# Taking the products of zeros out of the first microseconds of a one-core graph kernel

## What is computed

```python
edge_index = jnp.stack([src, dst])
x = _layernorm(x + _L0_gnn_ref(x, edge_index, ...))          # (x@W+b) spread three times over a 0/1 adjacency
x = _layernorm(x + _L1_gnn_ref(x, W, b, src, dst, 1024))     # sum of neighbours @ W.T + b
x = _layernorm(x + _L2_gnn_ref(x, wc, wn, bias, edge_index)) # x@wc + mean of (x@wn) over the edges + bias
x = _layernorm(x + _L3_gnn_ref(x, edge_index, ...))          # 8 heads of attention with softmax per target
```

## Time and profile before

| | |
|---|---|
| median of three executions | 392.14 us (391.53 to 392.75) |
| the profiled execution's own time | 390.91 us |
| its span, first to last instruction | 389.1 us |
| TensorE busy | 371.8 us (96%) |
| VectorE busy | 280.7 us (72%) |
| ScalarE busy | 239.8 us (62%) |
| GpSimd busy | 100.7 us (26%) |

### The profile page before, as it was taken

One profiled execution on the slowest core, in us unless ns is written; L12 is line 12 of the kernel. 1 busy time (PEld: TensorE's weight loads), 2 busy tenths in 40 slices (PEclk: granted clock), 3 DMA queues, 4 the chain that ended last, 5 costly groups with the idle time before them and its releaser, 6 DMA issues.

```text
span 389.1 us, 7789 instructions
## 1 busy us (share of the span) xinstructions
PE 371.8 (96%) x2721; PEld 218.3 (56%) x2721; DVE 280.7 (72%) x598; ACT 239.8 (62%) x415; POOL 100.7 (26%) x93
## 2 busy tenths in 40 slices
PE   6999989999999999999999999999899999999990
PEld 2455556544444444444444444444458889999990
DVE  8899999659986774207755446553795978999984
ACT  9999977575812355203661111467776999999344
POOL 5102000098800368100891000367200000112110
PEclk9999989999999999999999999999999999999997
DMA  5960060033000000000352000034202111210005
GB/s 166 385 221 1 0 217 3 3 109 107 2 0 0 0 2 3 0 2 0 72 91 54 0 0 2 14 81 83 40 1 113 55 56 70 95 57 3 3 5 219
DMA packets 27974, 22.70 MB, mean 58 GB/s; under 512 B 19552, under 2 KB 20768, under 8 KB 27936
## 3 DMA queue, kind: packets, MB, share of 16 engines
q1 hardware_dynamic: 27072, 19.06, 16.9%
q10 hardware_dynamic: 864, 3.15, 2.1%
HBM read 15.87 MB, written 2.13 MB: 46 GB/s over the span
## 4 chain that ended last, share of the span: by engine, by line
PE 88%; DVE 7%; issue 2%; ACT 1%; DMA 1%; DVEq 1%; POOL 0%; ACTq 0%; POOLq 0%
PE ps L764 20%; PE ps L1152 14%; PE ps L1093 8%; PE ps L1002 7%; PE ps L1043 7%; PE ps L956 7%; PE ps L965 7%; PE ps L811 7%; PE ps L931 4%; PE ps L946 4%; PE ps L832 2%; DVE c L1290 2%; PE ps L783 1%; DMA xTs<-big 1%; PE ps L882 0%
## 5 line engine op out<-in xcount | busy, mean ns | idle before, releaser
L764 PE MATMUL ps<-big,xTs 128*128 128x512 f16 x384 | 84.3, 379 | 0.3 <-DMA xTs<-big 0.3
L764 PEld LDWEIGHTS ps<-big,xTs 128*128 (+1 forms) x384 | 37.0, 98 | 43.8 <-issue 0.4
L673 ACT ACTIVATE big<-big,uvt 128x1024 bf16<-128x1024 f32 x55 | 58.5, 1141 | 0.0
L577 ACT ACTIVATE big<-xcur,nmr,rstd (+1 forms) x24 | 19.5, 813 | 34.0 <-DVE nmr L1420 34.0
L435 POOL TENSOR_TENSOR big<-xcur,big x16 | 18.5, 1157 | 60.2 <-ACT xcur L578 59.6
L811 PE MATMUL ps<-big,xTs 128*128 128x512 f32 x64 | 32.2, 603 | 0.0
L452 POOL TENSOR_TENSOR xcur<-xcur,c 128x512 f32<-128x512 f32 x6 | 7.1, 1185 | 89.4 <-DVE c L1623 89.4
L1093 PE MATMUL ps<-big,cst 128*128 128x260 f16 x256 | 29.8, 275 | 0.0
L469 ACT ACTIVATE big<-ps 128x512 f16<-128x512 f32 (+2 forms) x17 | 9.6, 567 | 31.6 <-PE ps L764 30.9
L405 POOL TENSOR_TENSOR big<-xTs,big 128x2048 f16<-128x2048 f32 x4 | 16.2, 4083 | 49.6 <-ACT big L469 49.6
L1002 PE MATMUL ps<-cst,big 128*128 128x512 f16 x128 | 27.8, 379 | 0.3 <-issue 0.3
(11 more groups left out here) (214 smaller groups left out, 710.8 us busy)
## 6 DMA issues: line engine op xcount, KB each, us to landing
big<-u_rows ACTq DMA_DIRECT2D x6, 512.0 KB, 3.6
xcur<-in_x SPq DMA_DIRECT2D x1, 2048.0 KB, 17.1
out<-xcur SPq DMA_DIRECT2D x8, 256.0 KB, 2.6
big<-in_W SPq DMA_DIRECT2D x1, 1024.0 KB, 6.1
xTs<-in_xT SPq DMA_DIRECT2D x1, 1024.0 KB, 10.1
big<-in_W3T SPq DMA_DIRECT2D x1, 1024.0 KB, 12.2
xTs<-in_W1T SPq DMA_DIRECT2D x1, 1024.0 KB, 5.4
xTs<-in_wc SPq DMA_DIRECT2D x1, 1024.0 KB, 8.8
```

Source lines behind the costliest of these rows:

```text
L673: act.activation(above[:, a % AHEAD, :], uf[:, h % 2], ACT.Relu, scale=BIG, bias=vb[:, j, h:h + 1]).then_inc(S["above_in"], 1)
L764: return mm(bank, lhs(k)[a], rhs(k)[b], start=start and k == 0 and n == 0, stop=stop and k == KT - 1 and n == 2)
```

## The change

The eight, one, four and twice two products of zeros (17 in all), the wait of TensorE on `blank_in` ahead of them, VectorE's memset of `blank`, the name `blank` and the constant `WARM` go. Nothing else is changed: no order, no bank, no other semaphore.

```diff
-WARM = (8, 1, 4, 2)
...
-        blank = ws[:, SLOT["W1"], 0, 0, :]
...
-            def warm(n):
-
-                for _ in range(n):
-                    mm(ps[:, 4, :], blank[:, 0:P], blank, start=True, stop=True)
-
-            pe.wait_ge(S["blank_in"], 1)
-            warm(WARM[0])
             pe.wait_ge(S["const_ready"], 4)
             pe.wait_ge(S["digits"], 1)
...
             ins.then_inc(S["tr"], 1)
-            warm(WARM[1])
             pe.wait_ge(S["prep"], F_KEY_IN)
...
             ins.then_inc(S["tr"], 1)
-            warm(WARM[2])
...
                 quad(q)
-                if q < H_FROM:
-                    warm(WARM[3])
...
-            dve.memset(blank, 0.0).then_inc(S["blank_in"], 1)
             dve.wait_ge(S["cols"], 2)
```

## The result

The kernel without the zeros is slower: 396.48 us (median of four executions, 395.75 to 397.33) against 391.85 us for the kernel before (four executions, 391.53 to 392.75). The two medians differ by 1.2%; the ratio estimated from all executions compared is 1.0094, with a 95% interval from 1.0050 to 1.0139.

What follows compares the result with a forecast made beforehand. TensorE bounds, busy 371.79 of 389 us. Terms: memset 0, turns 0, quad 6 late 0.85 (early start included), giving 391.8 on the profiled time, 393.0 on the median; plus 0.1, 393.1 us, range 391.6 to 394.8.

Steps and rivals of the forecast that it cites:

- the memset: VectorE's 0.27 us from 0.85 to 1.12; hidden by the wait for GpSimd's `first_i`, so removing it gains 0.
- the two turns: TensorE's L790 and L795 near the start: L790 up to 1.1 us sooner, but its readers are not; gain 0.
- The `h_part`s at the lower level: First `h_part`s before quad 6: 1.74 us each at the lower clock level, twice 0.87.
- Lateness at quad 6: TensorE's delay at quad 6, 0.85 us after 18.25, passes on in full through VectorE to the end.
- The early start of 0.85 us: Quad 2 through at about 11.25 instead of 12.12, so the first `h_part` starts 0.85 us sooner; TensorE's whole gain.
- The list: TensorE's `h_part`s, quads 3 to 5 and far columns laid out up to quad 6, which then starts at 19.1.
- The moment of the rise: TensorE's clock goes to the higher level between 14 and 17.5 us, middle 15.7, against about 11.5 before.
- Nothing there takes the delay back: After the last window, from L931 at 62.53, TensorE carries the chain and the delay from quad 6 stays.
- if the difference comes from behind 62.5 us: One of the signs, to be read in the changed trace, that the prediction is wrong.
- Slower by more: Rival: clock low for 7 to 9 us after 11.1, quad 6 1.8 to 2.7 us late, 394.0 to 394.9; chance 0.15.
- Hidden: Rival: clock rises at about 13.8, or early start and VectorE's lag cover the loss; 392.1 to 392.5; chance 0.22.
- Faster: Rival: clock up before the `h_part`s, quad 6 ready at 17.2, VectorE's 0.3 us of waits go; 391.8; chance 0.08.

Runs made afterwards that it cites:

- the two filled profiles: Changed kernel's start without zeros, both later sparse TensorE places given extra products, against the kernel before: memset kept (second run) 393.12 us; memset out 393.82 us.
- the filled test: Kernel before with all zeros, both later sparse places given extra products, plus 14 zero products (2.6 us) directly before quad 6: 393.79 us.
- the filled kernels: Extra TensorE products at 50 to 56 us and near 275 us; ratios to the kernel before: 0.9977 with start zeros, 1.0026, 1.0023 and 1.0029 without.
- the unfilled kernel with the delay: Kernel before, all zeros kept, plus 14 products of 448 columns of zeros directly before quad 6, later places unchanged: 397.23 us, ratio 1.0097.

## Why the prediction was wrong, point by point

**What was right.** At the start the memset lies beside GpSimd, and the two turns move nobody: L1248, which is `key16`, starts at 7.96 and was at 7.97. The `h_part`s at the lower level take about twice as long. Lateness at quad 6 passes on in full through VectorE to the end where the clock stays up: 2.22 at quad 6 and 2.24 in the span, 2.51 and 2.54, in the two filled profiles, and +2.65 for 2.6 in the filled test. No gain came back from the freed TensorE. The first part of the loss sits where the rise of the clock was named.

**The early start of 0.85 us was not there.** This is the step that failed by reasoning, not by size: "quad 2 ... could be through at about 11.25". I looked at its one-hots alone. `quad` also waits for a free bank, `win_free`, and the second window of quad 2 needs the add of window 1, which VectorE makes at 11.48, behind the one-hots that stand in its order. The chain above has it: DVE L1276 at 11.48, then L821 at 11.86, then the first `h_part` at 12.18. The zeros in TensorE's queue covered a wait that would have been there in any case. The list then starts at 12.15. With the rise at 15.7, as I had it, TensorE is at the lower level for 3.55 us rather than 4.4, and the sum is about +1.4 in place of +0.85.

**The moment of the rise was mis-sized.** I took 15.7 us, between 14 and 17.5, where the profiled execution of the changed kernel has 18.1. Without zeros at the start the profiles show 14.8, 14.9, 15.1, 15.2, 16.2, 16.9, 17.3, 17.6, 17.9, 18.1 and 18.2: eleven executions of one start, spread over 3.4 us, with the middle at 16.9. A list that starts at 12.15 gives about 2.0 us for that, and the profile that has its rise there has the add of quad 6 at 20.38, 1.98 late. Over the eleven this lateness goes from 1.0 to 2.7 us.

**What the clock does later was set at nothing.** By the profiles this is the largest step that failed: "Nothing there takes the delay back" is true, but something there adds to it, and I had named "if the difference comes from behind 62.5 us" as a sign of being wrong. In the kernel before, a low stretch near 56 us lay beside VectorE's chain. How long such a stretch lasts differs from one execution to the next: 3.4 us in the one I read, 6.8, 13.7 and 17.1 in others. Mostly it begins after TensorE's sparse work of 50 to 56 us, but in four profiles, one of them a filled kernel's, it begins between 63.9 and 65.5, where TensorE waits ahead of the first spreading step. The four profiles of the changed kernel, laid against the one of before (us; what a low stretch near 60 adds is read at the second eight products of that step, which started at 64.86 before):

| clock full from | quad 6's add late by | low stretch, and what it adds | pause near 276 longer by | span longer by |
|---|---|---|---|---|
| 18.1 | 2.6 | 55.6 to 62.4: 0.5; 280.9 to 284.3: 1.7 | 0.7 | 5.6 |
| 17.6 | 2.3 | 65.3 to 68.7: 1.9 | 0.7 | 4.7 |
| 14.9 | 1.1 | 55.9 to 69.5: 4.1 | 0.7 | 5.7 |
| 14.8 | 1.0 | 55.7 to 69.4: 4.1 | 0.7 | 5.7 |

(The columns add up to the span within 0.3.) The last one's low stretch:

```profile
55.70:69.40 13.70, 13.46 (x72) 10.65 (x73) 11.13 (x24) 6.77 (x8) 0.00 (x0) 0.50 0.20 71
69.40:80.00 10.60, 10.60 (x75) 5.75 (x73) 6.69 (x17) 4.65 (x5) 0.00 (x0) 1.00 0.00 1
```

The step there started at 66.03, 3.50 late where quad 6 was 1.0 late, and its first eight products ran at half clock, which costs 1.6 more. So in the two executions in which the clock rose early most of the loss is the later low stretch, and not the rise. By the medians: filling the two later places takes 1.9 us off the changed kernel (395.72 to 393.82) and 0.55 off the one before (391.69 to 391.14). The difference, 1.35, and the 2.7 of the start make the 4.0 that the change costs. With the ratios of the filled kernels the start's part would be some 2.0, and the later places' 2.0; the split is known to that only, as the filled kernels still have falls of the clock at the first step. Why the later places cost the changed kernel more is not shown: TensorE's code there is the same, and the times at which it is reached differ.

**The memset was set at 0.** At the start it is. But the 0.38 us of VectorE's longer wait near 278 us goes with it in every profile, and is about half of the 0.7 in the table's fourth column. I looked only at the place where the instruction stood.

The Trainium skill, page "TensorE: Matmul & The Clock Gate", section "A second HAM failure mode: psum-queue depth-cycling", tells of just this: TensorE pausing briefly and often between groups of products, while PSUM banks are cycled, lets the clock fall. This case's trace agrees. Between 50 and 56 us TensorE waits 0.2 to 0.35 us ahead of nearly each window, and the granted clock then falls to 0.5; with these waits filled it stays at 1.00 up to 62 us in all seven filled profiles. I had the row of the low stretch and wrote that it lies beside VectorE's chain; I did not ask what it costs when it is longer. The bound of below 1% that I quoted from the Trainium skill, same page, section "What's actually happening", is for the penalty of the ramp. The traces here agree with it: the late rise costs 1.0 to 2.7 us at quad 6, which is 0.3 to 0.7% of this kernel, and the whole loss is 1.0% because the clock is lost in more than one place.

**The rivals.** "Slower by more" came nearest, with 394.0 to 394.9, and got 0.15. Its lateness of 1.8 to 2.7 us at quad 6 is what two of the four profiles of the changed kernel have; but it knew that one mechanism alone, and 395.7 and 396.5 lie above it as well. "Hidden" is out: TensorE's lateness at quad 6 is visible in each of the eleven profiles without zeros. "Faster" is out.

**The reading of one profile.** The profiled execution of before took 390.91 us, near the lowest of the 134 measured later. Its low stretch was a short one. I took the difference of 1.23 us to the median as a constant, where it was a sign that executions differ, and the places in which they do belong into the range.

## What to carry to other kernels

Products that nobody reads can pay for themselves where TensorE would start its real work at the lower clock level; what they buy is read at the first place where another engine waits for TensorE, not in TensorE's own busy time. Before counting on work that "starts sooner", read every wait ahead of it, the free buffers as well as the operands. And where a trace shows a fall of the clock that costs nothing now, find out what it would cost if it were longer or came later: filling sparse stretches of TensorE with spare products made this kernel's times steadier (no execution above 393 us in 36, where the kernel before had 26 of 134 above 393.9), and no slower. Last, a total that changes by a microsecond is not yet the effect that was looked for: align the two traces and see where the time appears, as it did here at 150 and 276 us.

## What the hardware showed that I had not expected

The same program gets its higher clock at different times. With all the zeros at the start, or one more, the six profiles have it from 5.3, 5.7 (two of them), 6.2, 6.6 and 11.6 us on. The earlier rise brought no gain at quad 6: its add started at 18.49 to 18.55 in the three of the early ones that have no delay, and at 18.40 with the rise at 11.6. And a rise that comes early can be lost again: a fixed number of zeros is over sooner at the higher level. In the filled kernel with the delay the clock was full from 5.7 us and low again from 12.5 to 15.9, and the first `h_part`s ran slowly after all, which is the further 1.6 us by which its quad 6 was late (timeline; L785 are zeros, L838 quads, L817 `h_part`s):

```profile
9.48 0.60 PE L785 MATMUL ps<-big 128*128 128x512 f16 x2
10.47 0.35 PE L838 MATMUL ps<-adj,cts 128*128 128x88 f16 x4 [0.40 <-DVE cts L1299]
10.67 0.59 PE L785 MATMUL ps<-big 128*128 128x512 f16 x2
...
12.05 0.25 PE L838 MATMUL ps<-adj,cts 128*128 128x96 f16 x2 [0.56 <-DVE c L1311]
12.32 1.90 PE L817 MATMUL ps<-big,xTs 128*128 128x512 f32 x2
```

In the unfilled kernels the low level behind 50 us lasted between 3.4 and 17.1 us in the profiles, and TensorE can be busy for nearly all of a long one (13.63 of 13.70 us in the unfilled kernel with the delay).
